# A recommendation tower on one core: dense inputs padded to 128 rows, and the last layer's operands swapped in the loop

## The reference

```python
x0 = xk = e                                   # (1024, 39, 16)
for W in [f0, f1, f2]:                        # each gives 128 features
    z = jnp.einsum('bfd,bgd->bfgd', x0, xk).reshape(b, f * g, d)
    cur = jnp.einsum('bpd,pm->bmd', z, W)
    outs.append(cur)
    xk = cur
z = jnp.sum(jnp.concatenate(outs, axis=1), axis=-1)        # (1024, 384)
h = jnp.concatenate([z, dense_ctx], axis=1)                # (1024, 400)
h = jnp.maximum(h @ W_top1 + b_top1, 0.0)                  # 400 x 512
h = jnp.maximum(h @ W_top2 + b_top2, 0.0)                  # 512 x 256
y = h @ W_top3                                             # 256 x 1
```

## Time and profile before

| | |
|---|---|
| median of 3 runs | 1406.24 us (1405.4 to 1407.19) |
| the profiled execution, its own time | 1398.14 us |
| its span | 1396.1 us |
| TensorE busy | 1320.1 us, 95% |
| VectorE busy | 1125.4 us, 81% |
| ScalarE busy | 908.1 us, 65% |
| GpSimd busy | 703.1 us, 50% |
| mean granted clock | 0.98 of full |

### The profile page before, as it was taken

One profiled execution on the slowest core, in us unless ns is written; L12 is line 12 of the kernel. 1 busy time (PEld: TensorE's weight loads), 2 busy tenths in 40 slices (PEclk: granted clock), 3 DMA queues, 4 the chain that ended last, 5 costly groups with the idle time before them and its releaser, 6 DMA issues.

```text
span 1396.1 us, 20072 instructions
## 1 busy us (share of the span) xinstructions
PE 1320.1 (95%) x5856; PEld 992.7 (71%) x5856; DVE 1125.4 (81%) x2792; ACT 908.1 (65%) x3233; POOL 703.1 (50%) x697
## 2 busy tenths in 40 slices
PE   1199999999999999999999999999999999999998
PEld 0166766777777777777777777777777777777777
DVE  0279988888878888788878888788887888788874
ACT  1157777677666766667666776667666677667663
POOL 6786556654645466554556546454664532233200
PEclk8599999999999999999999999999999999999998
DMA  5271021100311021110211003110221102110000
GB/s 108 48 212 38 13 76 43 50 27 8 98 37 36 20 69 51 35 41 2 84 35 49 27 3 102 31 41 21 60 59 35 42 1 74 40 47 26 1 1 1
DMA packets 51355, 62.47 MB, mean 45 GB/s; under 512 B 12707, under 2 KB 24725, under 8 KB 51245
## 3 DMA queue, kind: packets, MB, share of 16 engines
q1 hardware_dynamic: 33644, 54.64, 12.7%
q0 software_dynamic: 10128, 2.98, 2.0%
q10 hardware_dynamic: 7473, 3.56, 1.0%
HBM read 10.02 MB, written 0.00 MB: 7 GB/s over the span
## 4 chain that ended last, share of the span: by engine, by line
PE 88%; DVE 4%; POOL 3%; ACT 2%; issue 2%; DMA 1%; SPq 0%; DVEq 0%
PE Y L740 20%; PE Y L742 19%; PE Y L741 19%; PE C L688 14%; PE C L702 5%; PE S L696 5%; POOL rows L331 3%; ACT Y L467 2%; PE C L720 1%; PE C L710 1%; PE C L711 1%; PE S L662 1%; DVE sum_b L607 1%; ACT h L474 1%; DVE sum_a L612 1%
## 5 line engine op out<-in xcount | busy, mean ns | idle before, releaser
L467 ACT ACTIVATE Y<-Y,x_col 128x128 f32<-128x128 f32 x2944 | 800.9, 356 | 402.8 <-PE Y L742 388.3
L740 PE MATMUL Y<-f_high,cur_high 128*128 128x512 f32 (+1 forms) x1280 | 627.7, 490 | 9.3 <-DVE part L620 4.6
L742 PE MATMUL Y<-f_high,cur_low 128*128 128x512 f32 (+1 forms) x1280 | 498.3, 389 | 0.0
L741 PE MATMUL Y<-f_low,cur_high 128*128 128x512 f32 (+1 forms) x1280 | 497.6, 389 | 0.0
L369 POOL TENSOR_TENSOR pairs<-shifted,base 117x512 f32<-117x512 f32 x186 | 240.3, 1294 | 471.5 <-PE C L688 469.6
L331 POOL DMA_INDIRECT rows<-in_tbl_dram,ids_sb x312 | 304.6, 976 | 77.0 <-issue 65.2
L740 PEld LDWEIGHTS Y<-f_high,cur_high 128*128 128x128 f32 x1280 | 241.0, 188 | 122.9 <-issue 46.3
L741 PEld LDWEIGHTS Y<-f_low,cur_high 128*128 128x128 f32 x1280 | 242.1, 189 | 92.3 <-issue 52.2
L742 PEld LDWEIGHTS Y<-f_high,cur_low 128*128 128x128 f32 x1280 | 240.3, 188 | 51.1
L607 DVE SCALAR_TENSOR_TENSOR sum_b<-Y,x_col,sum_b 128x128 f32<-128x128 f32 x768 | 262.6, 342 | 0.0
L688 PE MATMUL C<-pairs,f_sum 117*128 117x512 f32 (+1 forms) x448 | 230.0, 596 | 6.1 <-DVE pairs L570 6.1
(11 more groups left out here) (78 smaller groups left out, 649.2 us busy)
## 6 DMA issues: line engine op xcount, KB each, us to landing
shifted<-x_seq SPq DMA_DIRECT2D x157, 234.0 KB
base<-x_seq SPq DMA_DIRECT2D x95, 78.0 KB
rows<-in_tbl_dram,ids_sb POOLq DMA_INDIRECT x312
shifted<-x_seq SPq DMA_DIRECT2D x31, 156.0 KB
G<-in_L_rec_f_dram ACTq DMA_DIRECT2D x3, 832.0 KB, 9.1
w_sb<-in_W_top_dram SPq DMA_DIRECT2D x1, 768.0 KB
w_sb<-in_W_top_dram SPq DMA_DIRECT2D x1, 512.0 KB
shifted<-x_seq ACTq DMA_DIRECT2D x2, 234.0 KB
```

What stands on the lines that cost most here:

```text
L467: ins = act.activation(where[:, i * M:(i + 1) * M], where[:, i * M:(i + 1) * M], ACT.Copy, scale=x_col[:, t // JT % QG, t % JT, f:f + 1])
L740: pe.matmul(where, ch, wh, start=True, stop=False)
L741: pe.matmul(where, ch, wl, start=False, stop=False)
L742: pe.matmul(where, cl, wh, start=False, stop=True).then_inc(y_filled, 1)
```

## The change

`z_dense` and `w1_dense` get 128 rows instead of 16. VectorE sets both to zero at its start, and the load of the weights and the copy of the transposed inputs write the first 16 rows, after a wait for the zeros (`dense_zero`). The matmuls of L710, and the dense ones of the tail, so become 128 rows high, with zeros in 112 of them.

In `mlp3` of the loop h2 (128x128) becomes the stationary operand and the column of w3 the streamed one: the result is one column of 128 instead of one row. ScalarE copies the column to `y_col`, and the output transfer of the first seven batch tiles reads `y_col`, 896 elements of 4 bytes. The last layer of the tail stays as it was.

```diff
-        w1_dense = sb("w1_dense", [D, 512])
+        w1_dense = sb("w1_dense", [P, 512])
...
-        z_dense = sb("z_dense", [D, B])
+        z_dense = sb("z_dense", [P, B])
...
-        y = sb("y", [1, B])
+        y = sb("y", [1, P])
+        y_col = sb("y_col", [P, BT - 1])
...
-                    sp.dma_start(w1_dense[:], w1[3 * P:3 * P + D, :]).then_inc(mlp_in, 16)
+                    sp.wait_ge(dense_zero, 2)
+                    sp.dma_start(w1_dense[0:D, :], w1[3 * P:3 * P + D, :]).then_inc(mlp_in, 16)
...
-            sp.dma_start(out[0:B - P, :].rearrange("b o -> o b"), y[:, 0:B - P]).then_inc(y_out, 16)
+            sp.dma_start(out[0:B - P, :].rearrange("(t p) o -> p (t o)", p=P), y_col[:],
+                         allow_slow_non_contiguous=True).then_inc(y_out, 16)
             sp.wait_ge(y_ready, 1)
-            sp.dma_start(out[B - P:B, :].rearrange("b o -> o b"), y[:, B - P:B]).then_inc(y_out, 16)
+            sp.dma_start(out[B - P:B, :].rearrange("b o -> o b"), y[:]).then_inc(y_out, 16)
...
-                act.activation(z_dense[:, h * 512:(h + 1) * 512], Y[0:D, (4 + h) * 512:(5 + h) * 512],
+                if h == 0:
+                    act.wait_ge(dense_zero, 1)
+                act.activation(z_dense[0:D, h * 512:(h + 1) * 512], Y[0:D, (4 + h) * 512:(5 + h) * 512],
...
-                act.activation(y[:, bt * P:(bt + 1) * P], C[0:1, 0:P], ACT.Copy).then_inc(c_read, 1)
+                act.activation(y_col[:, bt:bt + 1], C[:, 0:1], ACT.Copy).then_inc(c_read, 1)
...
-            act.activation(y[:, B - P:B], S[0:1, 0:P], ACT.Copy).then_inc(y_ready, 1)
+            act.activation(y[:], S[0:1, 0:P], ACT.Copy).then_inc(y_ready, 1)
...
             dve.memset(f0_mirror[0:NF, 0, :], 0.0).then_inc(mirror_zero, 1)
+
+            dve.memset(z_dense[:], 0.0).then_inc(dense_zero, 1)
+            dve.memset(w1_dense[:], 0.0).then_inc(dense_zero, 1)
...
-                    ins = pe.matmul(C[0:1, 0:P], w3_sb[:, k:k + 1], h2[:, k, :], start=k == 0, stop=k == 1)
+                    ins = pe.matmul(C[:, 0:1], h2[:, k, :], w3_sb[:, k:k + 1], start=k == 0, stop=k == 1)
```

More of the change, by code:

```diff
@@ L197, in build @@
         f2_in, dense_in, mlp_in = sem("f2_in"), sem("dense_in"), sem("mlp_in")
+        dense_zero = sem("dense_zero")
         dense_filled, dense_read = sem("dense_filled"), sem("dense_read")
```

## The result

The changed kernel takes 1394.85 us (median of 7 runs, 1389.5 to 1399.2) against 1406.43 for the kernel before (7 runs): 0.9909 of it, 95% interval 0.9884 to 0.9935. The forecast was 1395.4. The profiled execution took 1389.5 us with a span of 1387.5, 8.6 us less than the one of before, not the 10.8 that the sum had off the profiled execution. This difference is worth following, because it is made of three stretches (start, middle, tail), and most of what the first and the last of them show isn't the change's.

What follows compares the result with a forecast made beforehand. TensorE was taken as the bound (95% busy, 88% of the chain); 9.9 us in the loop plus 0.9 in the tail, 10.8 off the 1406.24 median, gave 1395.4 us, range 1392.0 to 1399.5.

Steps and rivals of the forecast that it cites:

- the sum: Whole kernel: 9.9 us from seven MLPs in the loop plus 0.9 in the tail, 10.8 us gained.
- step 1: MLP's first layer: padding the dense product to 128 rows gains 0.57 and 0.78 us, together 1.35 us per MLP.
- step 2: MLP's last layer, operands swapped: 0.52 us becomes 0.46, gain 0.06 us per MLP.
- step 4: Loop tiles around an MLP: TensorE's gain reaches the end, with up to 4.95 us of room before VectorE bounds.
- VectorE takes half back: Rival, tiles after an MLP: VectorE catches TensorE, half of the 9.9 us is lost, 1400.3 us; chance 0.06.
- step 5: Tail, third dense group to G product: padding gains 0.9 us, or 1.1 at full clock.
- step 6: Start and output: memsets of about 2 us, waits for zeros and 896 four-byte output pieces all stay hidden.

Runs made afterwards that it cites:

- the four kernels above: Kernel before with the 16-row product last in each block, 64 rows, 96 rows, or two 16-row products adjacent: 1398.8, 1395.2, 1385.9, 1394.1 us; before 1396.5.
- zeros alone: Kernel before plus padded tensors, memsets and waits, matmuls still reading 16 rows, last layer as before: 1407.86 us, 0.9995 of before.
- padding alone: Kernel before with w1_dense and z_dense at 128 rows, last layer not swapped: 1396.88 us, 0.9921 of before.
- second rearranged start: The change with SyncE issuing the 49 mirrored f0 loads and VectorE adding them later, run again: 1386.49 us, 0.9917 of before.

## Why the prediction was right

**The padding** (step 1): 0.57 and 0.78 us for the two halves forecast, 0.58 and 0.77 measured. The counting by distances between starts carried over to the hundredth, because each of its prices came from the same kind of matmul in the same engine's queue. The price is that of a passage between heights, by the four kernels above: 0.21 to the first product of the other height instead of 0.11, and 0.21 from there to its second pass instead of 0.11. The traces give the size of the steps, 0.1 us at each change and 0.1 more for the weight load that isn't made ahead. The Trainium skill's rule (TensorEngine Tiling, Key Properties) that a change of tiling mode drains TensorE agrees with the place of the steps and with their absence between two 16-row products. The Trainium skill (TensorEngine Tiling, Available Configurations) lists modes of 32, 64 and 128 rows, so that 64 rows fit a lower mode and 96 need the full array. The two kernels fell on these two sides (2.71 and 1.94 us for the second half); the profile doesn't show the mode itself.

**The swap** (step 2): 0.06 forecast, 0.05 in the distance of the last layer. The sum came out by luck, since two of its terms were off and cancel: the first pass, forecast at 0.21 because its load stands bare, took 0.13, and the way to L749, forecast at 0.03, took 0.11. The two steps between were 0.11, as forecast: one streamed column kept the pace of 0.11. What the swap took away is the way out of L726, a product one column wide, 0.20 us before; the way out of a 16-row product takes the same 0.20, and in both cases the next weight load begins only at the change (L740's at 404.86). ScalarE's copy fell from 252 to 180 ns; nothing waited for it.

**Does it arrive** (step 4): yes, 1.46 a batch tile for 1.41, and 9.96 us in all for 9.9; the other five profiles of kernels with both parts of the change give 9.9 to 10.1. The rival in which VectorE takes half back would have shown 0.7.

**The tail** (step 5) is the term that was mis-sized: 0.9 us forecast, 0.24 measured at one clock. The working set the old stretch, of which most ran at half clock (2.45 us), against a new one partly at half clock. But at full clock the old stretch is 1.59 us (zeros alone) and the new one 1.35, held there by L632's reduction. A fall of 6.8 us slows whatever lies in it: what it takes from this place it takes from the next if it comes a little later. Whole tails show that, from chunk 0 of the last tile to the end. With a fall they take 31.8 us with 16 rows and 31.7 with 128; without one 28.9 with 64 rows and 28.8 with 96 or 128. So the padding is worth 0.1 there at either clock.

**What was added** (step 6): nothing that the times show, by the zeros alone. The traces show 0.3 us: in every profile with padded tensors, the zeros alone and the 64 rows among them, TensorE waits 0.4 us for VectorE's z before the sixth MLP, and that tile is 0.28 us longer by it than without them. Why is open. The 1024-column memset took 0.91 us and the 512-column one 0.48, 1.4 us for the estimate of 2. The output's 896 pieces were issued at 1351.4, 36 us before the end, and the tail is as long with them (31.7 us, the change's with a fall) as without (31.7, padding alone).

**The sum.** The traces account for 10.0 us in the loop and 0.1 to 0.2 in the tail, of 10.8 forecast. Measured were 11.6, 12.1 and 14.0 on three occasions. The excess was not forecast, and part of it is likely the clock in the tail, which only stood in the range. Of the six profiles in which the dense products have 16 or 64 rows, five have a fall to half clock in the tail, each with 31.8 us from the last tile's chunk 0 to the end; the one without has 28.9. Of the eight with 96 or 128 rows, two have it (31.7) and six have not (28.8). A fall costs 2.9 us, so that 5 of 6 against 2 of 8 would be worth (0.83 - 0.25) x 2.9 = 1.7 us on the mean.

The single executions bear on it by their mean granted clock. Where before took 1397.7 us beside the second rearranged start, two executions of before had a mean clock of 1.000, which leaves no room for a fall of 6.8 us, and took 1397.14 and 1397.22; two of the rearranged kernel had 0.999 and took 1386.65 and 1386.70. That is 10.5 us between executions without a fall in the tail, close to the traces, or up to 0.9 more if the rearranged ones had the short fall in tile 0 that two of their three profiles show. The medians there differ by 11.2. How much of the excess on the other chips is the clock stays open, and so does the cause. That the padding prevents the fall is argued from the counts, not shown: the 64-row kernel was spared too, and how long TensorE sat idle before the third dense group does not tell the cases apart (1.51 us in the changed kernel, without a fall, and 1.52 in the padding alone, with one; 0.85 in the kernel before, with one, and in the 64-row kernel, without).

The profiled pair hid 5.4 us of the gain through the start, and showed 2.8 and 0.9 too much through the clock. The forecast of the median, 1395.4 for 1394.85, was in part luck: the tail was put 0.7 too high, and 1.5 of the 11.6 us stands in no term of the forecast.

## What to carry to other kernels

Read matmuls by the distance between their starts and look for steps where neighbours differ in height: here (fp32, 128 columns, full clock) a product of 16 or of 64 rows between full ones cost 0.4 us for its two passages. Fill it with zeros beyond 64 rows (96 and 128 did equally well), or, where the padding can't be had, put such products next to each other so that they share one pair of passages. Before comparing two profiles, cut both at the same instructions (first tile, last tile) and settle start, middle and tail apart: here 5 us of start-up and 3 us of clock came and went with no part of the change.

## What the runs showed of the hardware

The issue of small loads has two speeds. ScalarE's 49 loads of 0.5 to 19 KB took 17.0 to 17.2 us in six profiles and 42.4 to 43.4 in five others, kernels with and without the change in both groups. On the chip where they were slow in all four profiles the kernel before ran at 1407.7 us, on those where they were quick at 1396.5 to 1398.7. Profiles taken together on one chip were alike in this, so it looks like a property of the chip or the moment and not of the kernel; its cause stays open. The first chunk comes 4.4 to 9.3 us later in the slow profiles than in the quick ones of like kernels, which is a part of the 9 to 11 us between the medians. The kernel before's own profile (17.2 us of issues, 1398.14 us) stands with the quick ones and the runs around its median of 1406.24 with the slow ones, which fits the 8.1 us between them.

Height has a threshold and no slope: 16 and 64 rows behave alike to 0.01 us, and so do 96 and 128. Width seems to have a price of the same kind: the way from a product one column wide to a full one took 0.20 us, where full ones need 0.03. One width only was run.
